# The adapter's down projection: fp32 matmuls on a scaled and shifted tile, or f16 products with the scale in a table for each expert

## What is computed

```
# layer 0, expert e = itok0[b]
h = gelu(x @ Wi[e] + bi[e])                   # 256 -> 1024
r = h @ Wo[e] + bo[e] + x                     # 1024 -> 256
z = (r - mean(r)) * rsqrt(var(r) + 1e-12)
y = z * gamma[e] + beta[e]
# layer 1, domain d = itok1[b]
a = gelu(y @ down_W.T + down_b)               # 256 -> 64
u = (a @ expert_W[d].T + expert_b[d] + domain_emb[d]) @ up_W.T + up_b
s = u + y
out = (s - mean(s)) * rsqrt(var(s) + 1e-5) * ln_gamma + ln_beta
```

## Time and profile before

| | |
|---|---|
| median of 3 runs | 499.2 us (499.18 to 499.23) |
| the profiled execution's own time | 498.85 us |
| its span | 497.1 us |
| busy: PE, ACT, POOL, DVE | 95%, 75%, 72%, 72% |
| granted TensorE clock over the span | 0.983 |
| a step in the middle | 6.68 us |

### The profile page before, as it was taken

How to read it: one execution, slowest core, us unless ns; L and a number is a source line. 1 busy time by engine, 2 the same in 40 slices (tenths; PEclk the granted TensorE clock), 3 DMA queues, 4 the chain that set the end, 5 groups by cost and what they waited for, 6 DMA issues and landing times.

```text
span 497.1 us, 19258 instructions
## 1 busy us (share of the span) xinstructions
PE 473.9 (95%) x5778; PEld 438.7 (88%) x5779; DVE 355.6 (72%) x936; ACT 373.8 (75%) x1099; POOL 358.6 (72%) x587
## 2 busy tenths in 40 slices
PE   4699999999999999999999999999999999999972
PEld 2399999999999999999999999999999999999961
DVE  6678777777777777777777777777777767666662
ACT  2588887777787778788777778877878877677651
POOL 6044787788778877788778877887778876667765
PEclk9799999999999999999999999999999999999996
DMA  4734343333343333333333333333343222222111
GB/s 117 269 83 117 93 91 105 100 95 99 102 106 105 86 99 100 98 96 103 103 88 95 99 100 99 102 86 102 97 100 79 63 55 66 64 58 55 39 44 32
DMA packets 70257, 45.84 MB, mean 92 GB/s; under 512 B 43969, under 2 KB 61778, under 8 KB 70098
## 3 DMA queue, kind: packets, MB, share of 16 engines
q1 hardware_dynamic: 69200, 45.25, 34.6%
q10 hardware_dynamic: 1026, 0.21, 0.2%
HBM read 36.51 MB, written 8.91 MB: 91 GB/s over the span
## 4 chain that ended last, share of the span: by engine, by line
PE 93%; DVE 3%; POOL 1%; issue 1%; DMA 0%; ACT 0%; POOLq 0%; DVEq 0%
PE p_h L929 13%; PE p_h L931 12%; PE p_h L930 12%; PE p_o L939 12%; PE p_o L938 12%; PE p_o L937 12%; PE p_d L948 7%; PE p_u L962 6%; PE p_t L970 3%; PE p_u L958 2%; PE p_o L1028 1%; PE p_h L872 1%; DVE W L737 1%; POOL y L475 0%; PE p_t L872 0%
## 5 line engine op out<-in xcount | busy, mean ns | idle before, releaser
L929 PE MATMUL p_h<-x_hi,W 128*128 128x128 f16 x1088 | 193.8, 220 | 0.0
L930 PE MATMUL p_h<-x_lo,W 128*128 128x128 f16 x1088 | 193.6, 220 | 0.0
L931 PE MATMUL p_h<-x_hi,W 128*128 128x128 f16 x1088 | 193.6, 220 | 0.0
L589 ACT ACTIVATE h<-p_h,bi_tile 128x128 f32<-128x128 f32 x544 | 152.6, 362 | 0.6 <-PE p_h L931 0.6
L938 PE MATMUL p_o<-W,h_hi 128*128 x544 | 148.3, 273 | 0.0
L939 PE MATMUL p_o<-W,h_lo 128*128 x544 | 148.3, 273 | 0.0
L937 PE MATMUL p_o<-W,h_hi 128*128 x544 | 148.3, 273 | 0.0
L492 POOL TENSOR_TENSOR rs<-mv,neg_half 128x1 f32<-128x1 f32 x68 | 59.7, 878 | 74.2 <-DVE mv L808 74.2
L929 PEld LDWEIGHTS p_h<-x_hi,W 128*128 x1088 | 107.0, 98 | 5.2 <-issue 3.8
L930 PEld LDWEIGHTS p_h<-x_lo,W 128*128 x1088 | 106.9, 98 | 2.1
L931 PEld LDWEIGHTS p_h<-x_hi,W 128*128 x1088 | 106.9, 98 | 0.0
(11 more groups left out here) (155 smaller groups left out, 814.3 us busy)
## 6 DMA issues: line engine op xcount, KB each, us to landing
stage<-in_w SPq DMA_DIRECT2D x56, 256.0 KB, 2.7
x_nat<-in_x SPq DMA_DIRECT2D x136, 64.0 KB, 2.1
out<-y SPq DMA_DIRECT2D x136, 64.0 KB, 2.0
x_T<-in_xT SPq DMA_DIRECT2D x134, 64.0 KB, 2.2
W<-in_w SPq DMA_DIRECT2D x8, 256.0 KB, 4.6
g_t<-in_gamma SPq DMA_DIRECT2D x1, 1024.0 KB, 7.8
W<-in_expert_W SPq DMA_DIRECT2D x2, 128.0 KB, 3.0
upT<-in_up_W SPq DMA_DIRECT2D x2, 64.0 KB, 2.7
```

The costliest lines, as they stand in the source:

```text
L589: ins = nc.scalar.activation(h[:, c, :], p_h[parity][:, c, :], ACT.Gelu, bias=bi_tile[:, parity, c:c + 1], scale=1.0 / (XS * WS))
L929: mm(p_h[parity][:, c, :], hi, x_hi[:, parity, k, :], start=(k == 0), stop=False)
L930: mm(p_h[parity][:, c, :], hi, x_lo[:, parity, k, :], start=False, stop=False)
L931: ins = mm(p_h[parity][:, c, :], lo, x_hi[:, parity, k, :], start=False, stop=(k == KD - 1))
```

## The change

Gamma moves out of `yT` and into the weights, beta into the bias of the gelu: y @ down_W.T = z @ (gamma[e] * down_W.T) + beta[e] @ down_W.T.

- A table `dtab` holds, for each of 8 experts and both halves k of the features, the high and low f16 parts of `downT` times gamma[e] times 512. ACT writes 16 high parts (`high_down`) and DVE 16 low parts (`low_down`), 6 of each in step 0, 6 in step 1, 4 in step 2.
- PE computes beta @ down_W.T for all experts with two fp32 matmuls of 8 columns into `p_t`, behind `c_tables(1)` and ahead of step 0. Since `p_t` still holds `u_s`, they wait for `u_ready`. DVE adds `down_b` and writes `dbias`.
- In each step ACT's two `yT` instructions become one copy of 256 columns into `z_hi` in f16, and DVE gets one more instruction at its step's end, `z_lo` = 8z - `z_hi`.
- `down` becomes six f16 matmuls of 128 columns instead of two fp32 ones, with four more `lower_ap` ahead of them, since the table's place hangs on the expert. The sort writes a fifth number for each step of PE.
- POOL copies one column of `dbias` for the gelu instead of four columns for `yT`. The gelu waits for it and has the scale 1/4096 and that bias.

The diff, cut to its core:

```diff
+        dtab = sb("dtab", [P, E0, KD, 2, P], f16)
+        dbias = sb("dbias", [P, E0])
+        dscale = sb("dscale", [P, E0, KD])
-        gb_tile = sb("gb_tile", [P, 2 * KD])
-        yT = sb("yT", [P, KD, P])
+        db_tile = sb("db_tile", [P, 2])
+        z_hi = sb("z_hi", [P, KD, P], f16)
+        z_lo = sb("z_lo", [P, KD, P], f16)
...  GpSimd, step
-                    need(pool, yT_done, i - 2)
-                    pool.tensor_copy(gb_tile[:, :], gb_c[:, bass.ds(e_before * 2 * KD, 2 * KD)]).then_inc(gb_done, 1)
+                    need(pool, a1_done, i - 3)
+                    pool.tensor_copy(db_tile[:, parity:parity + 1], dbias[:, bass.ds(e_before, 1)]).then_inc(db_done, 1)
...  ScalarE
+            def high_down(es):
+                for e in es:
+                    for k in range(KD):
+                        ins = nc.scalar.activation(dtab[:, e, k, 0, :], downT[:, k, :, :].rearrange("p u a -> p (u a)"),
+                                                   ACT.Copy, scale=dscale[:, e, k:k + 1])
+                ins.then_inc(d_hi, 1)
+            act.wait_ge(dscale_ready, 1)
...  in its step
-                    nc.scalar.activation(a1[:, :], p_d[:, 0:P], ACT.Gelu, bias=downb[:, :]).then_inc(a1_done, 1)
+                    act.wait_ge(db_done, i - 2)
+                    nc.scalar.activation(a1[:, :], p_d[:, 0:P], ACT.Gelu, bias=db_tile[:, 1 - parity:2 - parity],
+                                         scale=1.0 / (ZS * DS)).then_inc(a1_done, 1)
...
+                if isinstance(i, int) and i < 3:
+                    high_down(range(E0)[3 * i:3 * i + 3])
                 if exists(i - 2):
                     act.wait_ge(tr_done, i - 1)
-                    act.wait_ge(gb_done, i - 1)
-                    for k in range(KD):
-                        ins = nc.scalar.activation(yT[:, k, :], p_t[:, k * P:k * P + P], ACT.Identity,
-                                                   bias=gb_tile[:, KD + k:KD + k + 1], scale=gb_tile[:, k:k + 1])
-                    ins.then_inc(yT_done, 1)
+                    nc.scalar.activation(z_hi[:, :, :].rearrange("p k t -> p (k t)"), p_t[:, 0:D], ACT.Copy, scale=ZS)\
+                        .then_inc(zhi_done, 1)
...  VectorE, behind the sort
+            v.tensor_scalar(dscale[:, :, :], gb_c[:, :].rearrange("p (e r k) -> p e r k", r=2, k=KD)[:, :, 0, :], DS,
+                            None, ALU.mult).then_inc(dscale_ready, 1)
+            dve.wait_ge(d_summed, 1)
+            v.tensor_scalar(dbias[:, :], p_t[:, 0:E0], downb[:, 0:1], None, ALU.add).then_inc(d_bias, 1)
+            def low_down(es):
+                dve.wait_ge(d_hi, es[0] // 3 + 1)
...
...  at its step's end
+                if isinstance(i, int) and i < 3:
+                    low_down(range(E0)[3 * i:3 * i + 3])
+                if exists(i - 2):
+                    dve.wait_ge(zhi_done, i - 1)
+                    v.scalar_tensor_tensor(z_lo[:, :, :].rearrange("p k t -> p (k t)"), p_t[:, 0:D], ZS,
+                                           z_hi[:, :, :].rearrange("p k t -> p (k t)"), ALU.mult, ALU.subtract)\
+                        .then_inc(zT_done, 1)
...  TensorE
+            pe.wait_ge(u_ready, 1)
+            for k in range(KD):
+                beta_k = gb_c[:, :].rearrange("p (e r) -> p e r", r=2 * KD)[:, :, KD + k]
+                ins = mm(p_t[:, 0:E0], downT[:, k, :, :].rearrange("p u a -> p (u a)"), beta_k, start=(k == 0),
+                         stop=(k == KD - 1))
+            ins.then_inc(d_summed, 1)
...
-                    pe.wait_ge(yT_done, i - 2)
+                    pe.wait_ge(zT_done, i - 2)
                     if isinstance(i, int) and i == 3:
-                        pe.wait_ge(adapter_in, 6 * 16)
+                        pe.wait_ge(d_lo, 3)
                     for k in range(KD):
-                        ins = mm(p_d[:, 0:P], downT[:, k, :, :], yT[:, k, :], start=(k == 0), stop=(k == KD - 1))
+                        hi, lo = down_weights(k)
+                        mm(p_d[:, 0:P], hi, z_hi[:, k, :], start=(k == 0), stop=False)
+                        mm(p_d[:, 0:P], hi, z_lo[:, k, :], start=False, stop=False)
+                        ins = mm(p_d[:, 0:P], lo, z_hi[:, k, :], start=False, stop=(k == KD - 1))
                     ins.then_inc(down_done, 1)
...
                     if c == DOWN_AT and exists(i - 3):
+                        for k in range(KD):
+                            for part in down_weights(k):
+                                pe.lower_ap(part, for_matmul_weights=True)
                         down()
```

More of the change, by code:

```diff
@@ L19 @@
 AS, CS = 8.0, 512.0
+ZS, DS = 8.0, 512.0
 EPS0, EPS1 = 1e-12, 1e-5
@@ L230, in build @@
         tr_done = sem("tr_done")
-        gb_done = sem("gb_done")
-        yT_done = sem("yT_done")
+        db_done = sem("db_done")
+        zhi_done = sem("zhi_done")
+        zT_done = sem("zT_done")
+        dscale_ready = sem("dscale_ready")
+        d_summed = sem("d_summed")
+        d_bias = sem("d_bias")
+        d_hi = sem("d_hi")
+        d_lo = sem("d_lo")
         yg_done = sem("yg_done")
@@ L974, in up_weights @@
                     return ctab_flat[:, bass.ds(domains[n] + part * D, D)]
-                there, here, *domains = [
+                there, here, *domains, down_at = [
                     nc.s_assert_within(r, 0, top, skip_runtime_bounds_check_because="the sorting clips every index")
-                    for r, top in zip(indices(pe, 4 * i + IDX_PE, 4, DOMAIN_TOP), 2 * [PLACE_TOP] + 2 * [DOMAIN_TOP])]
+                    for r, top in zip(indices(pe, 5 * i + IDX_PE, 5, DOMAIN_TOP),
+                                      2 * [PLACE_TOP] + 2 * [DOMAIN_TOP] + [(E0 - 1) * DOWN])]
                 if exists(i):
```

30 lines of the change are left out of this document (23 added, 7 removed).

## The result

The changed kernel takes 500.31 us in the median (9 runs, 499.89 to 501.33), the kernel before 499.2 beside it. The ratio is 1.0026, with an interval of 1.0015 to 1.0036: 0.7 to 1.8 us slower. The forecast was 494.2, with a range that ended at 498.0. The profiled execution is one of 500.31 us, its span 498.6, which is 1.5 more than before.

The account below looks back on a forecast made before the run. PE's own work was taken to bound the kernel, with 93% of the chain. The span of 497.1 us, less 10.7 at `down`, plus 5.7 at the start, gave 492.1; the median was to go from 499.2 to 494.2, range 491.8 to 498.0.

Parts of the forecast that it names:

- `down` at 0.335: PE's six f16 matmuls take 0.335 us instead of 0.50, saving 0.165 a tile, 10.7 us over 65 tiles.
- rival 1: At `down`, only two passes are saved, 0.11 us a tile or 7.2 in all: 497.7 us; chance 0.09.
- ACT and DVE in the steps between at 0: In the steps between start and end, ACT's and DVE's changed work is off the path and costs 0.
- rival 5: In each step `z_lo` pushes DVE's `r` back; a step longer by 0.1 us gives 500.7 us; chance 0.03.
- The end at 0: From 480 us on the path runs through DVE and POOL, so the change costs 0, within 0.3 either way.
- The first product at 26.8: At the start PE's first product waits for `u_s` and register work: 26.8 us, 2.9 later than 23.90.
- the start: Up to step 3, PE's wait, the late clock and table parts on ACT and DVE cost 5.7 us, bounds 4.0 to 8.
- More register work ... I take nothing: Around `down`, four `lower_ap` and one more loaded number are done by PE's sequencer ahead of the matmuls: 0 us.
- Rival 4: PE's sequencer no longer stays ahead at `down`, between chunks 2 and 3: 0.30 us a tile, 513.7 us; chance 0.08.
- The clock's rise: At the start PE's clock goes to 2.4 GHz at 26.5, 30.0 or 31.4 us; the middle was taken.

Follow-up runs that it names:

- fifth_later: Changed kernel with beta matmuls and tables moved ahead (491.23 us), but PE loads four numbers at the step's head, the fifth behind `up`: 496.67 us.
- both_split: Changed kernel with beta matmuls and tables moved ahead (491.23 us), but PE loads two numbers at the step's head, three behind chunk 0: 502.41 us.
- packed: Changed kernel with beta matmuls and tables moved ahead (491.23 us), but the fifth number rides in the third, taken out by register operations: 489.78 us.
- hole_filled: Changed kernel with all table parts written ahead of step 0 (496.68 us), plus five unread fp32 matmuls in PE's gaps ahead of step 0: 496.4 us.
- beta_early: Changed kernel (500.31 us) with only the beta matmuls moved into PE's idle time ahead of round 1, writing `p_d`: 497.23 us.

## Why the prediction was wrong

**Right.** `down` at 0.335: measured 0.335, a saving of 0.165 (taken: 0.165), over all steps -10.7 (-10.7). So rival 1, two passes only (0.11), is out: what fp32 cost beyond its passes went too. ACT and DVE in the steps between at 0: `z_hi` 0.40 and `z_lo` 0.42 us, DVE's slack at 0.31; rival 5 is out. The end at 0: -0.1. The first product at 26.8: 26.97. That the start would cost, and through which chain (the tables ahead of `r`, then PE's wait): right.

**The step that failed: "More register work ... I take nothing".** It rested on two rows. The first, that matmuls around `down` follow without idle time, is true, and the four `lower_ap` there cost 0.2 us or nothing in the whole run. But the fifth number isn't loaded there. It is loaded at the step's head, and the trace of before has that load, 1.00 us for four numbers: 0.25 each, had I divided. In ordinary steps it is hidden; at a turn, the prediction itself had the 0.15 us of stall that says nothing is hidden there. Adding 0.23 at 13 turns would have given 3.0 us, and a forecast of 497.2, still inside its own range. The traces show 3.8 us lost up to step 68, and 2.7 of them are that load. Rival 4 named PE's sequencer, at the wrong place: it was priced at each `down`, where there is none, and not at each turn.

**The term that was mis-sized: the start, 8.5 in place of 5.7** (bounds 4 to 8). Of the 2.8 us, 1.7 are there when ACT's second batch ends, at 43.14 and not 41.4. Its first gelu starts 0.3 late, 0.2 of that with the first product. It then waits 0.6 for the second half of step 0's product, which ran at 1.2 GHz almost to its end, and 0.2 for DVE, whose first batch took 2.4 us and not 1.3. Its two batches take 1.75 and 1.88 where 1.5 were taken (0.29 from start to start, not 0.25). DVE's second batch adds 0.3 (1.6, not 1.3), so `r` starts at 44.75, not 42.7. From there to PE's bias matmul it is 0.7, not 0.4, and behind that 1.4 up to step 3 where 0.9 were taken; the clock's second fall, which the prediction doesn't have, is some 0.2 of this. Single prices for ACT were read from copies and gelus, none from a conversion with a scale per partition. The clock's rise was weighed at 26.5, 30.0 and 31.4, each 4.6 us behind some start of work. It came at 32.0, later than all three: one rise in one trace gave no rule.

Together +2.8 and +3.8, with -0.1 at the end, make the 6.5 between the forecast's -5.0 and the +1.5 of the span.

## What to carry to other kernels

A cost that is hidden in each step is not hidden at a loop's turn: list what the sequencer does between the branch and the first instruction of the next step, and price every number added there by the number of turns. And work that a change puts ahead of a pipeline's first steps belongs in idle time that the profile shows, with no wait for a buffer in between: here the place alone decided over 8.7 us, the difference between a loss of 0.3% and a gain of 1.6%; with the expert packed into a number that was loaded anyway, and half the turns, the gain is 2.2%.

## What the runs showed of the hardware

- PE's load of numbers from on-chip memory takes 0.31 us for one, 0.53 for two, 0.77 for three (`fifth_later`, `both_split`), 1.00 for four, 1.23 for five: about 0.23 us each and 0.08 in all. A second load after a turn is laid bare even behind `up`, while the register operations that `packed` adds cost some 0.02 us a turn.
- For four numbers and more these times hold where the first one's place in its table isn't a multiple of four. Where it is one, in steps 2, 6, 10 and so on, five numbers take 0.59 us (18 of 72 loads after) and four take 0.34 (18 of 72 in `fifth_later`). GpSimd's loads of five (0.57 and 1.17 us) and SyncE's of six (0.73 and 1.28) go the same way. The load of four in step 6 of `fifth_later`, and then that in step 5:

```profile
L278 PEldq TENSOR_LOAD <-idx x1: 337/337/337, 58.4 to 58.4; - x1
```

```profile
L278 PEldq TENSOR_LOAD <-idx x1: 1007/1007/1007, 51.9 to 51.9; - x1
```

  PE's part of the table starts at place 438, so that the loads at the turns, and all loads of the kernel before and of `packed`, are of the long kind. By this pattern two places of padding would make them short; from the two durations that is an estimate of 0.66 us less for each load of four. No run tries it.
- The rise of the clock came from 0.9 to 5.8 us behind the first product where nothing filled PE's gaps, and in `hole_filled` at 32.8 us although PE had been busy without a gap since 21.6. The second fall, at 45.6 in the changed kernel, came behind a wait of 2.01 us; in `beta_early` a wait as long at 39.9 was followed by none.
- ACT's conversion of 128 columns with a scale per partition takes 0.29 us from start to start in a batch of six, DVE's counterpart 0.26 in its second batch.
